# Gathers that skip indices past the table, in tiles filled beforehand with the table's last row

## The reference

```python
VOCAB, NUM_SAMPLED, NEG_INF = 125000, 1024, -1e9
inputs = front_emb[movie_id[:, 0]]                 # 2048 x 64
labels = target_movie_id[:, 0]
true_w, true_b = after_emb[labels], after_bias[labels]
samp_w, samp_b = after_emb[sampled_ids], after_bias[sampled_ids]
true_logits = sum(inputs * true_w, -1) + true_b - log(expected_count(labels))
sampled_logits = inputs @ samp_w.T + samp_b - log(expected_count(sampled_ids))
sampled_logits = where(sampled_ids == labels[:, None], sampled_logits + NEG_INF, sampled_logits)
logits = concatenate([true_logits[:, None], sampled_logits], 1)
loss = logsumexp(logits, 1) - logits[:, 0]
```

## Time and profile before

| | |
|---|---|
| runs shown, us | 83.03, 88.99, 82.94; median 83.03 |
| span of the profiled execution, first to last instruction | 79.0 us |
| what lies around that span in the profiled execution | not given by the page; the median lies 4.03 us above the span |
| busy, share of the span | VectorE 60%, ScalarE 59%, GpSimd 54%, TensorE 53% |
| gather queue | 1280 packets, 1.33 MB, 42.7% of the time of 16 DMA engines |
| mean granted clock of TensorE | 0.838 |

### The profile page before, as it was taken

One profiled execution on the slowest core, in us unless ns is written; L12 is line 12 of the kernel. 1 busy time (PEld: TensorE's weight loads), 2 busy tenths in 40 slices (PEclk: granted clock), 3 DMA queues, 4 the chain that ended last, 5 costly groups with the idle time before them and its releaser, 6 DMA issues.

```text
span 79.0 us, 638 instructions
## 1 busy us (share of the span) xinstructions
PE 42.1 (53%) x139; PEld 27.1 (34%) x139; DVE 47.2 (60%) x148; ACT 46.3 (59%) x74; POOL 42.3 (54%) x49
## 2 busy tenths in 40 slices
PE   0002599871059969253905605903996796769000
PEld 0002167140047655041604205503573565537000
DVE  0698886780071682648080093622965999998950
ACT  6049996712293092896084023079619895999770
POOL 7578686736868668578776868664680000000000
PEclk9999999998555899999999555555557999999995
DMA  0822121222344575968548689779689100000000
GB/s 7 221 65 33 18 34 17 29 25 17 25 25 18 25 24 18 30 19 21 24 23 30 20 18 29 20 18 33 21 18 30 4 0 8 0 0 0 0 0 4
DMA packets 1715, 1.91 MB, mean 24 GB/s; under 512 B 944, under 2 KB 944, under 8 KB 1712
## 3 DMA queue, kind: packets, MB, share of 16 engines
q0 software_dynamic: 1280, 1.33, 42.7%
q1 hardware_dynamic: 432, 0.55, 2.6%
HBM read 1.87 MB, written 0.01 MB: 24 GB/s over the span
## 4 chain that ended last, share of the span: by engine, by line
issue 26%; PE 21%; DVE 18%; ACT 10%; POOL 9%; another core or an unknown queue 8%; DMA 5%; DVEq 0%
POOL w_rows L219 9%; PE psum L291 8%; DVE psum L512 7%; PE psum L289 7%; ACT psum L339 6%; PE psum L290 5%; DVE masks L404 5%; DMA w_rows<-after,rows 3%; DVE xT L420 2%; DMA id_cols<-ids 2%; DVE lowest L512 1%; ACT masks L311 1%; PE psum L244 1%; DVE prod L521 1%
## 5 line engine op out<-in xcount | busy, mean ns | idle before, releaser
L512 DVE CUSTOM_DVE_ANT_0 psum<-psum,masks 128x1024 f32<-128x1024 f32 x16 | 19.7, 1231 | 16.4 <-PE psum L291 9.1
L289 PE MATMUL psum<-wT_high,xT 128*128 128x512 f32 x32 | 16.4, 511 | 21.3 <-issue 10.5
L339 ACT ACTIVATE psum<-psum,lowest 128x1024 f32<-128x1024 f32 x16 | 17.2, 1077 | 7.7 <-issue 5.2
L219 POOL DMA_INDIRECT t_rows<-after,rows x16 | 16.9, 1058 | 6.5 <-issue 4.7
L219 POOL DMA_INDIRECT x_rows<-front,rows x16 | 15.8, 990 | 6.9 <-issue 4.0
L289 PEld LDWEIGHTS psum<-wT_high,xT 128*128 128x128 f32 x32 | 7.1, 222 | 27.5 <-issue 21.2
L291 PE MATMUL psum<-b_parts,ones 128*128 128x512 f32 x32 | 14.8, 463 | 0.0
L290 PE MATMUL psum<-wT_low,xT 128*128 128x512 f32 x32 | 14.7, 460 | 0.0
L311 ACT ACTIVATE masks<-sample_ids,neg_label 128x1024 f32<-128x1024 int32 x9 | 10.3, 1140 | 3.1 <-DMA sample_ids<-sample_row 3.1
L334 ACT ACTIVATE xT<-psum 64x256 fp32r<-64x256 f32 (+1 forms) x9 | 3.0, 349 | 13.7 <-remote 7.4
L317 ACT ACTIVATE masks<-masks,ln_big 128x1024 f32<-128x1024 f32 x9 | 10.3, 1142 | 0.1
(11 more groups left out here) (78 smaller groups left out, 33.2 us busy)
## 6 DMA issues: line engine op xcount, KB each, us to landing
sample_ids<-sample_row SPq DMA_DIRECT2D x1, 512.0 KB, 3.9
x_rows<-front,rows POOLq DMA_INDIRECT x16
t_rows<-after,rows POOLq DMA_INDIRECT x16
w_rows<-after,rows POOLq DMA_INDIRECT x8
id_cols<-ids SPq DMA_DIRECT2D x1, 20.0 KB, 1.7
out<-loss SPq DMA_DIRECT2D x1, 8.0 KB, 1.4
```

The lines of the kernel that those rows point to most:

```text
L219: return pool.indirect_dma_start(dst, None, table, bass.IndirectOffsetOnAxis(ap=rows[:, col:col + 1], axis=0))
L289: nc.tensor.matmul(o, x, wT_high[:, part], start=True, stop=False)
L339: nc.scalar.activation(logits(t), logits(t), ACT.Exp, bias=lowest[:, 0, t:t + 1], scale=-1.0, accum_out=sums[:, t:t + 1]).then_inc(exp_ok, 1)
L512: V.tensor_tensor_reduce(out=logits(t), in0=logits(t), in1=masks[:, t, :], scale=1.0, scalar=3e38, op0=ALU.add, op1=ALU.min, accum_out=low ...
```

## The change

Two new inputs hold the last row of each table, repeated 16 times (the row of `front` with a 1 behind it, the row of `after` with its bias). SP copies them to all partitions of `x_rows` and `t_rows` with two broadcast transfers of 4160 bytes per partition (520 KB each). Every gather gets the bound 124,999 and leaves out, without an error, an index above it, so the filled row stays. Label and movie indices are no longer clipped from above, which splits the instruction of L426 in two. GpSimd waits for both fills before its first x gather. The memset of the column of ones goes, since the fill brings it.

```diff
             sp.dma_start(sample_ids[:, :], sample_row.rearrange("(a n) -> a n", a=1).to_broadcast([P, SAMPLES])
                          ).then_inc(row_in, 16)
+            sp.dma_start(x_rows[:, :, :].rearrange("p t c -> p (t c)"),
+                         front_last.rearrange("(a n) -> a n", a=1).to_broadcast([P, TILES * AUG])).then_inc(last_in, 16)
+            sp.dma_start(t_rows[:, :, :].rearrange("p t c -> p (t c)"),
+                         after_last.rearrange("(a n) -> a n", a=1).to_broadcast([P, TILES * AUG])).then_inc(last_in, 16)
             sp.wait_ge(loss_ok, 1)
...
-            pool.memset(x_rows[:, :, EMBED], 1.0).then_inc(consts_ok, 1)
...
                 return pool.indirect_dma_start(dst, None, table,
-                                               bass.IndirectOffsetOnAxis(ap=rows[:, col:col + 1], axis=0))
+                                               bass.IndirectOffsetOnAxis(ap=rows[:, col:col + 1], axis=0),
+                                               bounds_check=VOCAB - 1, oob_is_err=False)
 
             pool.wait_ge(rows_ok, 1)
             for j in range(SAMPLE_TILES):
                 gather(w_rows[:, j, :], after, j).then_inc(w_in[j // 2], 16)
+            pool.wait_ge(last_in, 32)
             for g in range(len(X_GROUPS)):
...
-            link(V.tensor_scalar(wrapped[:, :], id_cols[:, :], float(-VOCAB), float(VOCAB - 1), ALU.max, ALU.min))
+            V.tensor_scalar(wrapped[:, LAB:], id_cols[:, LAB:], float(-VOCAB), None, ALU.max)
+            link(V.tensor_scalar(wrapped[:, 0:LAB], id_cols[:, 0:LAB], float(-VOCAB), float(VOCAB - 1),
+                                 ALU.max, ALU.min))
             V.tensor_tensor(rows[:, :], wrapped[:, :], wrap[:, :], ALU.add).then_inc(rows_ok, 1)
...
+    last = np.concatenate([arrays["front"][-1], np.ones(1, np.float32)])
+    arrays["front_last"] = np.concatenate([last] * TILES)
+    arrays["after_last"] = np.concatenate([arrays["after"][-1]] * TILES)
```

More of the change, by code:

```diff
@@ L34, with log_uniform_loss @@
 LN2_LOW, LN2_HIGH = -0.00021219444, 0.6933594
-def log_uniform_loss(nc, ids, sample_row, front, after, out):
+def log_uniform_loss(nc, ids, sample_row, front, after, front_last, after_last, out):
     f32, f32r, i32 = mybir.dt.float32, mybir.dt.float32r, mybir.dt.int32
@@ L156, in log_uniform_loss @@
         rows_ok = sem("rows_ok")
+        last_in = sem("last_in")
         consts_ok = sem("consts_ok")
@@ L237, in _ @@
             pe.wait_ge(ident_ok, 1)
-            pe.wait_ge(consts_ok, 3)
+            pe.wait_ge(consts_ok, 2)
             def turn_w(q):
@@ L340, in exps @@
                                      accum_out=sums[:, t:t + 1]).then_inc(exp_ok, 1)
-            act.wait_ge(consts_ok, 3)
+            act.wait_ge(consts_ok, 2)
             act.wait_ge(row_in, 16)
@@ L527, in _ @@
             dots_done = 0
-            dve.wait_ge(consts_ok, 3)
+            dve.wait_ge(consts_ok, 2)
             for t in range(TILES):
```

## The result

The changed kernel took 75.0 to 88.42 us, median 76.66; the kernel before, in the same comparison, 82.94 to 89.42, median 86.01. The ratio is **0.907**, 95% interval 0.892 to 0.922, so it is faster. This ratio compares only the two fastest runs of each kernel, 75.0 and 75.57 against 82.94 and 83.03 us, because the others are spread too widely (the medians of all four would give 0.891). The forecast was 63.1 us, range 59.5 to 73.0: the direction was right, the size was far off, and the time lies outside the range.

A forecast was written before the change was run, and what follows sets the result against it. Late TensorE signals, tied to reads of one table row, were taken to bound the kernel. Without them GpSimd's gather chain ends the span at 59.05 us instead of 79.0, so 83.03 - 20.0 = 63.1 us, range 59.5 to 73.

The forecast's parts named there:

- the coincidence: 16 to 60.5 us: TensorE's late signals begin and end with last-row reads; VectorE idles 23.7 us in 22 to 60.5.
- rival 1: Tile loop, 16 to 60 us: late signals have another cause and stay, about 83 us, within 2%; chance 5%.
- Skipped reads, a landing 1.5 us after the gather: x and label gathers: about 7 of 8 descriptors disappear; rows land 1.5 us after GpSimd finishes, like the samples'.
- Start of the scores: Start of the tile loop: with prompt signals the first reduction starts at about 19.9 us.
- Tiles 0 to 7, and compute alone: Tile loop: reduction of tile 8 starts at 38.4 us, and compute alone would end at 56.9 us.
- GpSimd as the bound: Gather chain at 1.25 us pitch: last label gather starts at 52.2, end at 58.95, 2 us behind compute.
- The bound: Index bound in each gather instruction: no change in duration taken, between shrinking to 0.30 us and 0.97 us more.
- The two fills: Start: two 520 KB fills land by 13.1 us, hidden by sample gathers; priced at nothing, 1 us if cover fails.
- 2 (low clock): Tile loop: TensorE stays at half clock, 72.6 us; chance 4% for the whole length, 11% for partial clock or lateness.
- 3: Gathers with the bound: skipped rows are still read, 83 us or somewhat more by the fills; chance 2%.
- 4: GpSimd's gathers: the bound lengthens each, up to 101.7 us; 6% slower, 8% for 0.1 to 0.3 us extra (67 to 75).
- 5: GpSimd's gathers get shorter and compute becomes the bound, 61.0 us; chance 16%.

The follow-up runs named there:

- e8_again: Kernel before with the last row spread over 128 adjacent copies and one-input masks, no bound or fill, on a late-signal chip: 93.1 to 94.9 us.
- e3_fourth: Changed kernel without x and label gathers, filled rows standing for all of them, on a late-signal chip: 58.26 us.
- after_third: Changed kernel, unchanged, run again on a late-signal chip: 75.39 to 89.91 us.
- the second comparison: Kernel before and changed kernel again, with further variants, on a prompt-signal chip: 70.35 us before, 66.86 us changed, ratio 0.947.
- after_again: Changed kernel, unchanged, run again on a prompt-signal chip: 66.86 us, ratio 0.947.
- e1: Kernel before with x and label gathers using the samples' scattered indices, no fill or bound: 64.21 us, ratio 0.912.
- e3: Changed kernel without x and label gathers, filled rows standing for all of them, on prompt-signal chips: 58.27 us, ratio 0.828.
- e4: Changed kernel, fills and bound kept, with the samples' indices for x and label rows so nothing is skipped: 66.58 us.
- e9: Kernel before with the two fills and GpSimd's wait for them, but no bound, on a late-signal chip: 77.27 to 90.38 us.
- the first comparison: Changed kernel against the kernel before, on a late-signal chip: median 76.66 against 86.01 us, ratio 0.907.
- the fourth: Comparison on a late-signal chip: kernel before 81.16 to 89.35 us, changed kernel 75.39 to 89.91 us, no ratio given.
- the pacing: GpSimd's later gathers wait for earlier reductions, late-signal chip: 71.25 us added to the changed kernel, 74.87 us added to the spread-row, one-input-mask version.
- before_again: Kernel before, unchanged, run again on a prompt-signal chip: 70.35 us.
- e7: Kernel before with 127 copies of the last row behind each table and indices clipped per partition, no bound or fill: 64.11 us, ratio 0.923.
- e5: Changed kernel with the bound on x and label gathers alone, none on the sample gathers: 65.93 us, ratio 0.938.
- e6: Changed kernel with VectorE's masks made by an instruction with one SBUF input instead of two: 65.41 us, ratio 0.943.

## Why the prediction was wrong

**The step that failed** is the conclusion from the coincidence: "The lateness begins with the reads of the last row and ends with them", so that it would go with these reads. In the trace of before two things began and ended together, the reads of one row and GpSimd's x and label gathers. I named only the first. The sample gathers seemed to clear the second, since signals were prompt beside them. The profile after has nearly no reads of that row left and a wait of 26.6 us. e8_again has the gathers without the reads, and signals are later than ever (93.3 us); e3_fourth has neither and they are prompt (58.26 us); pausing GpSimd lets them through. Shown is: on such a chip TensorE's signals can be held back for as long as x and label gathers follow each other, and come within 3 us of their stopping. Not every signal beside gathers is late: the first eight gathers do little harm, and in after_third's quick execution some 17 x and label gathers don't either. Not told apart are GpSimd's own work, the few transfers of the gathers (DMA share 0.12 in e8_again) and their semaphores, since every edit adds or removes them together; nor is a late signal told apart from a matmul that really ends late, since its recorded end is modelled. What sets the lateness off, by which path it works, and why only some chips show it, stays open. I had rival 1 at 5%, and it was near the truth: another cause, though some gain.

The rule that I set against my forecast (the Trainium skill, "SBUF — State Buffer", section "SBUF: two separate sides") says that DMA traffic and engines don't slow each other. The runs agree as far as they go: with a queue share of 3.4% instead of 42.7% the lateness stayed. They don't show that the gathers' transfers have no part in it.

**The steps with prompt signals** can be read off the second comparison, where 63.1 us forecast stand against 66.86.

- *Skipped reads, a landing 1.5 us after the gather.* Right: the fifteenth label gather of after_again ends at 56.56 and its dot starts at 58.12.
- *Start of the scores.* First reduction forecast at 19.9; 19.89 in e1, 21.41 in after_again, where the bound has delayed everything.
- *Tiles 0 to 7, and compute alone.* Tile 8 forecast at 38.4, 37.75 in e1; end of compute at 56.9, 56.3 to 56.5 in e3.
- *GpSimd as the bound.* Right in kind: the dots wait 5.6 us for label rows in after_again. Wrong in size: the last gather starts at 56.86, not 52.2. Of these 4.7 us the later start of the first gather is 0.8 (4.15 against 3.38; 0.64 of it is the bound, the rest the indices that were ready later), the pitch 39 x 0.056 = 2.2, gathers that stood still beside masks 1.1 (0.40 + 0.16 + 3 x 0.18), a longer wait before the third x gather 0.5.
- *The bound.* I took no change between -0.64 and +0.97 us; it is 0.056 us per gather, 2.2 us over 39 pitches, and 0.64 us once. This mis-sized term alone is 2.8 us. (Between e1 and e4 only 1.8 us of it remain, since in e1 gathers stood still for 1.5 us longer beside masks.)
- *From span to time.* I added 4.03 us to the span, a median of other executions against the span of the profiled one; around the spans here lie 1.8 to 2.2, 2.2 in after_again. So the sum closes as 59.05 + 4.7 = 63.7 us of span, which after_again's profiled execution had, and 65.9 us of time; its median is 0.9 higher.
- *The two fills.* Hidden, as forecast (13.39 in e9).
- *Packets.* A gather has 32 packets (1280 for 40), half of them under 512 bytes, not the 16 that I named as a sign. The sums go by packets counted, so nothing else changes.
- *Rivals.* 2 (low clock) occurs beside late signals: the granted clock is 0.50 at 33 to 66 us of the profiled run, where TensorE works 10.0 of 33 us. 3 fell: skipped rows cost 0.02 us a packet in the queue. 4 came true with a smaller extra, 0.056 us, than the 0.1 to 0.3 of its mild form. 5 fell.

Where the gain comes from on a prompt chip: reads of one row 6.6 us (e1), less 1.8 us for the bound (e4 against e1), less up to 1 us that after_again (65.93 to 66.86) has over e4 (65.95 and 65.99, on another chip). Skipping itself gives nothing over reading scattered rows; the spread copies gain 5.3 us (69.45 to 64.11) and pay no bound. On the chips with late signals the first comparison had 0.907 and the fourth no clear difference; there the pacing is worth more than the change.

## What to carry to other kernels

When one thing in a trace begins and ends together with a stall, list everything else that does so too, and ask which single edit keeps one and drops the other; here that would have been scattered rows with the same gathers. Measure on more than one chip before a gain of this size is ascribed to a mechanism. A gather queue that many indices drive to one row was cured most cheaply here by copies of that row, and GpSimd, if its gathers are the bound, must be counted per instruction: 0.056 us each is 2.2 us over 39 steps.

## What the runs showed of the hardware

- On three of six comparisons' chips, TensorE's semaphores reached the waiting engines up to 26.6 us after the recorded end of the matmul while GpSimd issued indirect gathers (after), and in the same traces other signals beside gathers were prompt (after_third up to 40 us). Those of ScalarE and VectorE were not seen to be late (35.49 to 35.52 in e8_again).
- 128 gathered rows of 256 or 260 bytes go in 32 packets. These take 0.55 us each if 7 of 8 rows are the same one (before_again), 0.11 us if they are scattered (e1) and 0.08 us if the repeated row is spread over 128 adjacent copies (e7).
- A bound on an indirect gather costs 0.056 us each, and 0.64 us ahead of the first one in after_again; in e5, where gathers without a bound go first, that part doesn't show.
- A gather that starts inside one of VectorE's masks with two inputs from SBUF ends 0.88 us after the mask, 1.61 and 1.80 us instead of 1.00 (e5). The Trainium skill, "SBUF — State Buffer", section "Who interferes with whom", says that such an instruction of VectorE contends with a GpSimd instruction that reads SBUF; the trace agrees if a gather counts as one, which it doesn't show. It is not the whole cause: a mask with one input stopped a gather in the same way (1.40 us in e6).
